# Two GRU layers with a mixture of experts on one core: r's sums in a bank of their own, the mixture in groups of 128 steps, expert weights spread by DMA

## What is computed

```python
mixed = tanh(einsum('bte,he->bth', x, W_in) + b_in + ctx)
def step(h, xt):                      # one GRU layer; xt = mixed @ Wih.T + bih
    hr, hz, hn = split(h @ Whh.T + bhh, 3)
    r = sigmoid(xr + hr); z = sigmoid(xz + hz)
    n = tanh(xn + r * hn)
    return (1 - z) * n + z * h
h2 = gru(gru(mixed, layer 0), layer 1)
x = x + ((1 + sigmoid(gate)) * h2) @ W_out.T + b_out
# mixture, per token, over the new x
shared = (silu(x @ w1) * (x @ w3)) @ w2
s = sigmoid(concat(x, cond) @ router_W)      # 8 experts, the best 2 by s + bias
routed = sum_e combine_e * (gelu(x @ W1e[e]) @ W2e[e])
out = x + (shared + routed) / 3
```

## Time and profile before

| | us |
|---|---|
| median of three runs | 2289.26 |
| profiled execution, its own time | 2288.8 |
| its span | 2286.9 |
| TensorE busy in the span | 2162.7 (95%) |
| VectorE busy | 1844.0 (81%) |
| ScalarE busy | 1225.0 (54%) |
| GpSimd busy | 551.1 (24%) |

### The profile page before, as it was taken

How to read it: one execution, slowest core, us unless ns; L and a number is a source line. 1 busy time by engine, 2 the same in 40 slices (tenths; PEclk the granted TensorE clock), 3 DMA queues, 4 the chain that set the end, 5 groups by cost and what they waited for, 6 DMA issues and landing times.

```text
span 2286.9 us, 118156 instructions
## 1 busy us (share of the span) xinstructions
PE 2162.7 (95%) x47852; PEld 1359.9 (59%) x47852; DVE 1844.0 (81%) x11318; ACT 1225.0 (54%) x6577; POOL 551.1 (24%) x2444
## 2 busy tenths in 40 slices
PE   6888999999999999999999999999999999999987
PEld 2445566666566566666666566666666666566555
DVE  3778888888888888888888888888888888888874
ACT  3455555555555555555555555555555555555542
POOL 1222222222222222222222222222222222222220
PEclk9999999999999999999999999999999999999999
DMA  5000000000000000000000000000000000000000
GB/s 208 3 2 3 3 6 3 3 6 3 6 3 4 5 4 6 4 5 4 3 6 4 5 4 3 6 4 5 4 6 3 3 6 3 6 4 3 6 3 7
DMA packets 8483, 21.48 MB, mean 9 GB/s; under 512 B 1264, under 2 KB 5376, under 8 KB 7680
## 3 DMA queue, kind: packets, MB, share of 16 engines
q1 hardware_dynamic: 7936, 13.93, 1.7%
HBM read 11.83 MB, written 2.10 MB: 6 GB/s over the span
## 4 chain that ended last, share of the span: by engine, by line
PE 54%; DVE 28%; ACT 14%; issue 3%; DMA 0%; SPq 0%; POOL 0%; DVEq 0%; POOLq 0%; ACTq 0%
PE bank L309 42%; PE bank L259 9%; DVE bank L361 8%; ACT factors L418 8%; DVE cells L382 8%; DVE n_first L362 7%; ACT cells L422 7%; DVE z_pre L363 4%; PE bank L290 3%; DVE bank L371 1%; DVE hid L615 0%; PE bank L562 0%; DMA x_t<-in_x_t 0%; SPq L717 0%; PE bank L283 0%
## 5 line engine op out<-in xcount | busy, mean ns | idle before, releaser
L309 PE MATMUL bank<-w_h,cells 128*22 128x192 f32 (+4 forms) x32768 | 1763.6, 333 | 110.1 <-DVE cells L382 83.6
L309 PEld LDWEIGHTS bank<-w_h,cells 128*22 128x22 f32 (+4 forms) x32768 | 866.0, 113 | 787.4 <-DVE cells L382 657.5
L454 POOL TENSOR_SCALAR cells<-cells 128x4 f32<-128x4 f32 x2048 | 462.5, 226 | 1686.6 <-DVE cells L382 1685.3
L416 ACT ACTIVATE n_second<-bank 128x4 f32<-128x4 f32 x2048 | 361.9, 177 | 866.8 <-DVE bank L361 856.5
L382 DVE TENSOR_TENSOR_SCAN cells<-factors,cells 128x18 f32<-128x18 f32 x2048 | 401.2, 196 | 367.7 <-ACT cells L422 325.7
L361 DVE STREAM_TRANSPOSE bank<-bank 128x64 f32<-128x64 f32 x2048 | 519.3, 254 | 39.5 <-PE bank L309 39.5
L362 DVE STREAM_TRANSPOSE n_first<-bank 128x64 f32<-128x64 f32 x2048 | 534.2, 261 | 0.3
L418 ACT ACTIVATE factors<-z_pre 128x4 f32<-128x4 f32 x2048 | 429.5, 210 | 149.8 <-DVE z_pre L363 2.0
L363 DVE STREAM_TRANSPOSE z_pre<-bank 128x64 f32<-128x64 f32 x2048 | 428.6, 209 | 0.0
L371 DVE TENSOR_TENSOR_SCAN bank<-n_first,n_second 128x12 f32<-128x12 f32 x2048 | 400.9, 196 | 1.1 <-ACT n_second L416 1.1
L422 ACT ACTIVATE cells<-bank 128x8 f32<-128x8 f32 x2048 | 367.1, 179 | 5.2 <-DVE bank L371 0.2
(11 more groups left out here) (87 smaller groups left out, 601.2 us busy)
## 6 DMA issues: line engine op xcount, KB each, us to landing
x_t<-in_x_t SPq DMA_DIRECT2D x4, 512.0 KB, 6.6
w_1e<-in_w_1e SPq DMA_DIRECT2D x1, 2048.0 KB
w_2e<-in_w_2e SPq DMA_DIRECT2D x1, 2048.0 KB
out_y<-y SPq DMA_DIRECT2D x16, 128.0 KB, 2.2
w_x<-in_w_x SPq DMA_DIRECT2D x2, 768.0 KB, 8.0
w_h<-in_w_h SPq DMA_DIRECT2D x2, 768.0 KB, 9.7
w<-in_w SPq DMA_DIRECT2D x3, 512.0 KB
w_in<-in_w_in SPq DMA_DIRECT2D x1, 256.0 KB, 2.6
```

Of the source, the lines that this page charges most:

```text
L309: mm = pe.matmul(gates[l][p][32 * g:32 * g + B * (j + 1), 0:3 * U], state_tile(l, j, kt), w_h[l][:, kt, g, :], start=False, stop=False, ti ...
L416: act.activation(n_second[l][p][:, own, :, 0], r_pre[l][:, own], ACT.Tanh, scale=0.5).then_inc(s["for_n"], 1)
L454: pool.tensor_scalar(cell_part(step_rows(l, j), 3), cell_part(step_rows(l, j), 1), 0.5, None, ALU.mult)\
```

## The change

- r's sums get banks 0 and 1 (`r_sums`, both parities of a layer in one bank), those of n and z banks 2 and 3 (`nz_sums`). `recur` first makes r (64 columns, signalled by a semaphore `r`), then n and z (128 columns). Since two parities share a bank, projections wait until VectorE has read it (`turn`), and the biases come in two activations (r at j = 1, n and z at j = 2). Projections are cut into an r piece and two n, z pieces.
- VectorE has r's transpose as an instruction apart, into SBUF: for layer 0 at the slot's start, ahead of layer 1's state scan; for layer 1 behind layer 0's state scan. ScalarE is split likewise into `act_r` and `act_zn`, with mixture work between them.
- The mixture's group is 128 steps (256 tokens), `LAG` is 20 and `MLAG` 153. Matmul pieces have 256 columns, stand in part 0 alone, and are 94 a group; VectorE has 83 operations a group (large ones cut to 128 columns), ScalarE 22. Gating of the history on GpSimd is spread over four steps.
- `comb_t` goes to DRAM and comes back broadcast to all partitions (1 MB) by two transfers of SyncE; the spreading matmuls, copies and `pick` are gone. In the table of places `comb_t` stands 7 slots before the first weighting (slots 43 and 50), the second transfer 3 slots after `comb_t`.
- The input mixing is cut into 256-column pieces in free slots.

```diff
-BODY = 4 * CH
-LAG = CH + 3
+BODY = 8 * CH
+LAG = CH + 4
...
-MLAG = BODY + LAG + 4
+MLAG = BODY + LAG + 5
...
-def projection_pieces():
-    return {8: (0, 0), 10: (0, 1), 1: (1, 0), 2: (1, 1)}
...
+def projection_pieces(l):
+    return {8: (R, None), 10: (A, 0), 12: (A, 1)} if l == 0 else {1: (R, None), 2: (A, 0), 3: (A, 1)}
...
+    def transfer(self, name, after, took):
+        self.when[name], self.engine[name], self.value[name] = self.when[after] + took, "spread", 32
...
-        at = ((h // 2 + MLAG) % CH, h % 2)
+        j, part = (h // 2 + MLAG) % CH, h % 2
         if engine == "pe":
-            return at[1] == 0 and at[0] in projection_pieces()
+            return part == 1 or j in projection_pieces(1)
         if engine == "act":
-            return at in ((1, 0), ((1 + LAG) % CH, 1))
-        return at in ((12, 0), (2, 0))
+            return ((j - LAG) if part else j) % CH in (1, 2)
+        return (j, part) in ((13, 0), (3, 1))
...
-        gates = [[banks[2 * l + p] for p in range(2)] for l in range(2)]
-        acc = banks[4][:, 0:KT * TG].rearrange("p (m n) -> p m n", m=KT)
...
+        r_sums = [[banks[l][:, p * U:(p + 1) * U] for p in range(2)] for l in range(2)]
+        nz_sums = [[banks[2 + l][:, p * 3 * U:(p + 1) * 3 * U] for p in range(2)] for l in range(2)]
+        acc = banks[4][:, :].rearrange("p (m n) -> p m n", m=KT)
...
-            if j == 0:
-                pe.wait_ge(sets[l][1 - p]["xn"], 1)
...
             for kt in range(KT):
                 for g in range(NQ):
-                    mm = pe.matmul(gates[l][p][32 * g:32 * g + B * (j + 1), 0:3 * U], state_tile(l, j, kt), w_h[l][:, kt, g, :],
+                    mm = pe.matmul(r_sums[l][p][32 * g:32 * g + B * (j + 1)], state_tile(l, j, kt), w_h[l][:, kt, g, 2 * U:],
+                                   start=False, stop=False, tile_position=(0, 32 * g), skip_group_check=True)
+            mm.then_inc(s["r"], 1)
+            if j == 0:
+                pe.wait_ge(sets[l][1 - p]["xn"], 1)
+            if j == 3 and places_biases(t):
+                pe.wait_ge(s["bias"], 2)
+            for kt in range(KT):
+                for g in range(NQ):
+                    mm = pe.matmul(nz_sums[l][p][32 * g:32 * g + B * (j + 1), 0:2 * U], state_tile(l, j, kt),
+                                   w_h[l][:, kt, g, 0:2 * U],
                                    start=False, stop=False, tile_position=(0, 32 * g), skip_group_check=True)
             mm.then_inc(s["pe"], 1)
...
+        def project_at(pe, l, s, staged):
...
+            if piece == R:
+                pe.wait_ge(sets[0][p]["pool"], staged)
...
+                if t >= 0:
+                    pe.wait_ge(sets[l][p]["turn"], 2 * (t % CH) + 1)
+                project_r(pe, l, 1 - p)
+            else:
+                if t >= 0:
+                    pe.wait_ge(sets[l][p]["turn"], 2 * (t % CH) + 2)
+                mm = project_zn(pe, l, 1 - p, kt)
+                if kt == KT - 1:
+                    mm.then_inc(sets[l][p]["x"], 1)
...
                 if t0 is not None:
                     recur(pe, 0, t0)
...
+                if s in MIXING:
+                    mix_input(pe, *MIXING[s])
+                if j in projection_pieces(1) and CH <= s < T + CH:
+                    project_at(pe, 1, s, 1)
                 mixture_at(pe, "pe", s, 0, base)
                 if t1 is not None:
                     recur(pe, 1, t1)
+                if j in projection_pieces(0) and s < T - CH:
+                    project_at(pe, 0, s, 2)
                 mixture_at(pe, "pe", s, 1, base)
...
+        def dve_turn_r(v, l, t):
...
+            v.wait_ge(s["r"], j + 1)
...
+            v.transpose(r_pre[l][:].rearrange("p i b -> p b i"), blocks(r_sums[l][p])).then_inc(s["turn"], 1)
...
...
             s = sets[l][p]
...
-                v.wait_ge(s["go"], 1)
-            v.transpose(r_pre[l].rearrange("p i b -> p b i"), blocks(gates[l][p][:, 2 * U:3 * U])).then_inc(s["turn"], 1)
-            v.transpose(n_first[l][:, :, :, 2].rearrange("p i b -> p b i"), blocks(gates[l][p][:, 0:U])).then_inc(s["for_n"], 1)
...
+                if t0 is not None:
+                    dve_turn_r(v, 0, t0)
                 if 0 <= s - 1 - LAG < T:
                     dve_h(v, 1, s - 1 - LAG)
                 if t0 is not None:
-                    dve_turn(v, 0, t0)
+                    dve_turn_nz(v, 0, t0)
                     dve_n(v, 0, t0)
...
                 mixture_at(v, "dve", s, 0, base)
...
                 if t0 is not None:
                     dve_h(v, 0, t0)
                 if t1 is not None:
-                    dve_turn(v, 1, t1)
+                    dve_turn_r(v, 1, t1)
+                    dve_turn_nz(v, 1, t1)
                     dve_n(v, 1, t1)
...
                 mixture_at(v, "dve", s, 1, base)
...
+            if j == 1 and places_biases(t):
+                act.activation(r_sums[l][1 - p], biases[l][:, 3 * U:], ACT.Identity).then_inc(s["bias"], 1)
...
-            if j == 1 and places_biases(t):
-                act.activation(gates[l][1 - p][:, 0:NGATE * U], biases[l][:], ACT.Identity).then_inc(s["bias"], 1)
...
+            if j == 2 and places_biases(t):
+                act.activation(nz_sums[l][1 - p], biases[l][:, 0:3 * U], ACT.Identity).then_inc(s["bias"], 1)
...
                 if t0 is not None:
-                    act_step(act, 0, t0)
...
-                    mixed_tanh(act, mixing_at(s - 1)[0])
+                    act_r(act, 0, t0)
...
                 mixture_at(act, "act", s, 0, base)
+                if t0 is not None:
+                    act_zn(act, 0, t0)
                 if t1 is not None:
-                    act_step(act, 1, t1)
+                    act_r(act, 1, t1)
...
                 mixture_at(act, "act", s, 1, base)
+                if t1 is not None:
+                    act_zn(act, 1, t1)
...
-                        if t1 and t1 % BODY == 0:
-                            pool.wait_ge(now, 1)
-                            gate_history(pool, ROWS + t1 * B - TG, now)
+                    if t1 >= BODY and t1 % BODY < KT * B:
+                        group = t1 // BODY * BODY
+                        if t1 == group:
+                            pool.wait_ge(sets[1][0]["pool"], 1)
+                        gate_history(pool, ROWS + group * B - TG, t1 - group, sets[1][0]["pool"])
...
+                if m % BODY == mix.when["comb_t"] // 2:
+                    wait_for(sp, "comb_t")
+                    sp.dma_start(weights[:], comb_t[0:E, :]).then_inc(m_sets[mix.half("spread")]["spread"], 16)
+                if m % BODY == mix.when["comb_t"] // 2 + 3:
+                    sp.wait_ge(m_sets[mix.half("spread")]["spread"], 16)
+                    sp.dma_start(c_all[:], weights[:].partition_broadcast(P)).then_inc(m_sets[mix.half("spread")]["spread"], 16)
...
         def weigh(u):
...
-                    mix.add("dve", f"hid{u}" if m == KT - 1 else f"hid{u}_{m}", (f"act{u}", f"down{u - 2}") + ((f"gates{i}",) if i < 2 else ()),
...
+                    for q in range(2):
+                        mix.add("dve", f"hid{u}_{m}{q}", (f"act{u}_{m}", f"down{u - 2}") + (("spread",) if i == m == q == 0 else ()),
...
+        mix.transfer("spread", "comb_t", 12)
...
-        for q in range(2):
-            for i in range(4):
-                mix.add("pe", f"spread{q}{i}", () if i else ("comb_t", f"act{SH + q}"),
```

More of the change, by code:

```diff
@@ L40, in places_biases, with mixing_pieces @@
     return CH <= t < T - CH
-def projection_pieces():
-    return {8: (0, 0), 10: (0, 1), 1: (1, 0), 2: (1, 1)}
+R, A = 0, 1
+def projection_pieces(l):
+    return {8: (R, None), 10: (A, 0), 12: (A, 1)} if l == 0 else {1: (R, None), 2: (A, 0), 3: (A, 1)}
+def mixing_pieces():
+    free = [s for s in range(1, BODY) if s % CH > 3]
+    pieces = [(i, q, kt) for i in range(KT, KT * B * T // TB) for q in range(2) for kt in range(KT)]
+    return dict(zip(free, pieces))
 class Mixture:
@@ L56, in __init__, with add @@
         self.when, self.value, self.engine = {}, {}, {}
-    def add(self, engine, name, waits, issue, beside=False):
+    def transfer(self, name, after, took):
+        self.when[name], self.engine[name], self.value[name] = self.when[after] + took, "spread", 32
+        assert self.half(name) == self.half(after)
+    def add(self, engine, name, waits, issue, beside=False, even=False):
         last = self.ops[engine][-1][0] if self.ops[engine] else -1
@@ L63, in add @@
         h = max([self.when[w] + gap(w) for w in waits] + [last + (0 if beside else 1)])
-        while self.busy(engine, h):
+        while self.busy(engine, h) or even and h % 2:
             h += 1
@@ L497, in pool_slots @@
                     pool.wait_ge(s_hist, 1)
-                    gate_history(pool, ROWS + T * B - TG, s_hist)
+                    for piece in range(KT * B):
+                        gate_history(pool, ROWS + T * B - TG, piece, s_hist)
         def sp_slots(sp, s0, n, base):
@@ L594, in nonlinear @@
```

(5 more changed lines are left out.)

213 lines of the change are left out of this document (112 added, 101 removed).

## The result

The changed kernel takes 2264.09 us, the median of 4 runs (2255.13 to 2268.09), against 2289.24 us of the kernel before beside it: a ratio of 0.9884 (95% interval 0.9851 to 0.9916), 25 us or 1.2% faster. The prediction was 2137 us with a range of 2085 to 2245: the direction is right, the time lies outside the range, and five sixths of the gain did not come.

The account below looks back on a forecast made before the run. One layer's own loop latency, 2.143 us a step, was taken as the bound. Start 19.7, 1043.4 x 1.97 = 2055.5 and end 60.5 gave span 2135.7, adjusted to 2138 and stated as 2137 us, range 2085 to 2245.

Parts of the forecast that it names:

- The step: Recurrence step: 2.14 - 0.22 (r apart) + 0.01 (weight loads) + 0.04 (projections, activations, hand-overs) = 1.97 us.
- no loss: On TensorE, 192-column groups split into 64 and 128 still stream in 0.65 us; 0.01 charged, bounds 0 and +0.22.
- the third rival: r's matmuls on TensorE paced one by one at 28 ns, 0.45 instead of 0.22: 2377 us, slower; chance 0.09.
- The end: After the last state scan nothing hides the twice as big last group: 60.5 us, against 33.8 before.
- the forecast's allowance of 0.04 for the mixture and the hand-overs: Added per step: 0.01 projection steps, 0.01 activations between layer 1's r and z tanh, 0.02 hand-overs between layers.
- r's gain: r's transpose and tanh hidden; n's scan 0.36 instead of 0.58 after the matmuls' end E, 0.22 less per step.
- r's price in columns: TensorE time per layer and step: r's 64 columns 0.22 us, n and z 0.44; a 256-column mixture piece 0.44.
- The first rival: Larger mixture pieces show, a third getting through the in-order queues: step 2.05, 2221 us; chance 0.21.
- The second: Early r buys nothing because something else is as late: step 2.12 to 2.14, 2295 to 2315 us; chance 0.09.
- Spreading by DMA: Two transfers replace 64 matmuls and 8 copies, hidden during the recurrence; in the last group 2.2 + 5.9 = 8.1 us.

Follow-up runs that it names:

- e5: The kernel before with the changed kernel's mixture (groups of 128 steps, 256-column pieces, weights spread by DMA), r still together with n and z: 2324.63 us.
- e8: The changed kernel with 16 more TensorE waits at the end of each slot, on a load that ended long ago: 2661.13 us.
- e4: The kernel before with each mixture matmul of 128 columns cut into two of 64: 2308.23 us.
- e10: The changed kernel with the 128 columns of n and z made as 64 and 64: 3215.43 us.
- e11: e5 with its mixture matmuls on the whole array at once: 2459.74 us.
- e12: The kernel before with 16 more TensorE waits a slot, on a load that ended long ago: 2410.28 us.

## Why the prediction was wrong

**What failed.** The step is the term "no loss" in r's price on TensorE, and behind it the sentence against the third rival, that "the eight in 0.22 with their loads are 13.6 ns already". That reads a burst as a rate that can be kept up all step long. The earlier trace rows shows 16 instructions in 0.22, but before had only 92 a slot, one per 23 ns on average, so no step in its trace had asked for 145. Only its last group came near, with two blocks in a row of 3.49 us each and no pause, too short a stretch to tell. The text had the number (144 per step, 13.7 ns each) and took it as harmless because it was as fast as the fastest burst, when it should have asked what the average supply is. The average supply makes 145 x 14.5 ns = 2.1 us a step, not 1.97, and a row of before that would have raised the question is the instruction queue's: 375 blocks of 256 in 2287 us, which the change multiplies by 1.58.

**In the sum.** Between the first state scan of layer 0 (19.66) and the last of layer 1 (2206.95) lie 2187.3 us, 1043.4 x 2.096 instead of 1043.4 x 1.97 = 2055.5: 131.8 too little. The end was 56.5 instead of 60.5: 4.0 too much. 2137 + 131.8 - 4.0 = 2265, the profiled execution.

The supply's pauses are not all of it. Steps of layer 0 in the changed kernel, told apart by whether a pause of over 0.2 us at the block's edge falls into them (a step is counted here from 0.3 us before one state scan to 0.3 us before the next; counted from scan to scan the means without a pause are about 0.01 longer):

| changed kernel | steps | mean, us | steps with a pause, their mean | mean of those without |
|---|---|---|---|---|
| both layers, no mixture yet (82 to 322 us) | 120 | 2.003 | 6, 2.348 | 1.985 |
| both layers and mixture (339 to 2115 us) | 842 | 2.110 | 188, 2.382 | 2.032 |

Of the 0.140 us by which a step with mixture exceeds 1.97, 188 / 842 x 0.350 = 0.078 comes with the pauses. The other 0.062 stands in steps that have none: 0.015 is there without the mixture, 0.047 comes with it. So the forecast's allowance of 0.04 for the mixture and the hand-overs was too small as well, and what makes the 0.047 (the larger pieces, hand-overs, or shorter delays of the supply) stays open. In the kernel before the mixture costs a step nothing (2.145 before it starts, 2.142 with it).

**r's gain was right.** The clean step is 1.95, and where layer 1 runs alone at full clock its steps are 1.93 to 1.97; the forecast had 1.92 to 1.97. The gain is about 0.20 instead of 0.22, since n's scan comes at E + 0.41 and not 0.36, while r, n and z together take 0.86 from the first load to E instead of 0.89: n's transpose takes 0.28 to 0.31 instead of the 0.26 of the earlier trace rows. The tanh of z and that of n stand 0.14 apart, as taken.

**r's price in columns was right.** 0.22 in the chain for 64 columns, 0.44 for n and z, 0.43 for a mixture piece, as said. Within a burst four strips of 64 columns are 0.056 us apart and single instructions 6 to 7 ns. So the third rival's mechanism, 28 ns from matmul to matmul, is not there, and the earlier trace rows (four matmuls on one tile) doesn't carry over to four strips. The floor of about 25 ns for 1 to 64 columns that the Trainium skill gives ("TensorE: Matmul & The Clock Gate", section "Back-to-back issue gap") is met on one tile (the last three of the four in the earlier trace rows start 25 ns apart) but not here: 16 in 0.22 are 14 ns each. The third rival's direction was wrong too, but its condition was near: it decided from 2.115 us a step on, and the steps measured 2.097. With the end as measured the limit is (2289 - 19.7 - 56.5 - 1.9) / 1043.4 = 2.12, and two more instructions a slot would have used up the gain.

**The first rival** (2221, larger pieces show) has too small a time: the supply's pauses were not in it. Its cause is not refuted. e5 has the larger pieces with 0.007 us a step more than before, but its step of 2.15 leaves them 0.18 us more room than the forecast's 1.97; in the changed kernel the steps without a pause take 2.03 with the mixture, 0.02 under this rival's 2.05. **The second** (early r buys nothing) is refuted by the clean steps.

**Spreading by DMA.** Hidden as said: in the whole run VectorE waits once for it, in the last group, where nothing covers it. Timeline of the changed kernel's end, beside the earlier trace rows:

```profile
2226.79 0.28 SPq L582 DMA_DIRECT2D weights<-comb_t  x1
...
2228.10 0.34 SPq L585 DMA_DIRECT2D c_all<-weights  x1
...
2232.78 1.70 DVE L687 TENSOR_TENSOR hid<-act_t,c_all 128x128 f32<-128x128 f32 x8 [6.02 <-DMA c_all<-weights]
```

From the first transfer to the weighting it is 6.0 us, 4.7 of it the broadcast of 1 MB; the forecast had 8.1 and 5.9.

**What nobody had put in.** The last two steps take 2.47 and 2.60 us although little else runs, because the granted clock is at its lower level there, 1.2 GHz (0.50), after TensorE had been less busy since 2160 (TensorE busy 21.8 of 30 us from 2160 to 2190):

```profile
2204.00:2207.00 3.00, 2.40 (x44) 1.84 (x48) 1.13 (x7) 0.85 (x5) 0.23 (x1) 0.50 0.02 5
```

Groups of 128 columns start 0.213 us apart in it, 0.109 at full clock. It costs about 1.1 us here, and some 2.4 in e5's last four steps. At the start, right after the wait for the inputs, five of layer 0's first steps take 2.46 to 2.57, again at the lower level (granted clock 0.55 from 20 to 33 us), about 3 us in all.

## What to carry to other kernels

Before cutting matmuls into smaller ones, count the engine's instructions per step and divide the step by them. A burst in the trace shows what the array can take; only a long stretch with as many instructions shows what can be brought, and two blocks in a row are too few. In these kernels TensorE was held to one instruction per 14.3 to 14.8 ns on average, while bursts ran at 6 to 8. "Issue" pauses at one fixed place in every 256 instructions are its mark.

When two parts of a change use and spare the same resource, neither can be judged alone: here each was slower than the kernel before, and the pair was faster.

## What the runs showed of the hardware

- TensorE's instructions come in blocks of 16.4 KB, 256 instructions; five kernels that ask for more got one per 3.79 to 3.85 us of run time (594 to 849 blocks), and where TensorE paused for a block, one per 3.74 in the median (e8, with waits added, 4.22 of run time). The instructions of one block pass in 1.99 us in e4's last group. Nothing seems to be saved up in easier stretches: in e10 layer 0 alone asks for one instruction per 19 ns over 20 slots, and the second slot after layer 1 joins already takes 2.9 us.
- Short matmuls in four column strips are not held to a fixed time each: 64 columns pass in 0.056 us for four strips, loads of 14 columns 7 ns apart.
- A piece on the whole array or on two strips of 64 between work on four strips of 32 costs 0.30 to 0.34 us beyond its four-strip form (0.63 and 0.58 instead of 0.43 for 256 columns, and 0.36 instead of 0.22 for r behind it); over a kernel 135 us for some 740 such pieces (e11 against e5).
- 16 waits in a row in TensorE's program reach it as 8 or 9 instructions, and these stand 0.106 us apart even when their semaphore has long been reached (e8, e12).
